# How often GpSimd waits for free slots of the gather ring in the second layer's pass over the edges

## Chip, cores and metric

One NeuronCore of a Trainium2 chip runs the whole program in one launch. The metric is the device time in microseconds. The program is made of Bass instructions: each engine (TensorE or PE, VectorE or DVE, ScalarE or ACT, GpSimd or POOL, SyncE or SP) has its own list, in its own order, and the lists meet only in semaphores.

## What is computed

Two graph-attention layers, each with a residual and a layer norm around it, over 6250 nodes of 128 features and 106250 edges sorted by destination. The change lies in the second layer's pass over the edges, which computes this part of the reference:

```python
x_src = (node_embeddings @ W_src + b_src).reshape(num_nodes, H, D)      # H = 4, D = 32
x_dst = (node_embeddings @ W_dst + b_dst).reshape(num_nodes, H, D)
e = edge_emb[edge_type].reshape(-1, H, D)
combined = jax.nn.leaky_relu(x_src[src] + x_dst[dst] + e, negative_slope=0.2)
logits = jnp.einsum('ehd,hd->eh', combined, att)
mx = jax.ops.segment_max(logits, dst, num_segments=num_nodes)
ex = jnp.exp(logits - mx[dst])
sums = jax.ops.segment_sum(ex, dst, num_segments=num_nodes)
attn = ex / jnp.maximum(sums[dst], 1e-12)
agg = jax.ops.segment_sum(x_src[src] * attn[..., None], dst, num_segments=num_nodes)
```

`x_src[src]` is a gather: for each edge, one row of 132 numbers (528 bytes) is fetched from a table in HBM.

## The kernel before

The program runs in stages: preparing and first tables (`front`), the first layer's pass over the edges (`edges0`), joining and node updates (`join_tiles`, `nodes0`), the second layer's pass (`edges1`), and again joining and node updates (`join_tiles`, `nodes1`).

`edges1` goes over 896 steps of 128 edges. Four steps (QS = 4) make a quad, so there are 224 quads. All five engines run the same loop over quads, each with its own part. Sixteen quads (RQ = 16) are written out in the body of a hardware loop; the first 32 and the last 16 quads stand outside of it. `nth(i, c, per, plus)` turns a quad's number into the count that a semaphore has by then.

The gathered rows live in a ring of 16 quad slots, the tile `rows` (carved from `pair`, the name that the profile shows). A quad passes through it in this way:

- GpSimd, function `gather` (L1803 to L1814): for quad c it waits, at every eighth quad, for the index tile that ScalarE copies (`idx_in`, L1805), then until the slot is free (L1807, `sums`), then adds one to the semaphore `passed` (`apart`, L1808 and L83), for which nobody waits, and issues four indirect DMAs (L1811), one for each step. Each counts up the slot's semaphore `rows_in` by 16 when its rows have landed.
- TensorE, function `edge` (L1976 to L1988): when the slot's rows are in, it adds gathered and destination rows in PSUM (L1985, L1987) and counts `x_summed`.
- VectorE makes logits of them (L1851 to L1870); every eight quads a block of logits is turned, scanned, exponentiated and copied into the last four columns of the rows (L1997, L1891, L1898, L1905, ScalarE L1962, TensorE L2004, ScalarE L1944).
- Ten quads after its logits (LAG = 10), VectorE scales the quad's rows (L1867, semaphore `scaled`) and TensorE sums them into nodes with eight fp32 matmul passes (L2011) in two halves, h = 0 and 1. Each half counts `sums` by one, so quad w is done with its slot when `sums` is 2(w + 1). Each half has one PSUM tile, so TensorE waits before each half of a quad until ScalarE has copied out the same half of the quad before (L2009, semaphore `evicted`).
- ScalarE copies both halves out (L1953); VectorE adds them to the accumulators (L1880).

In iteration c TensorE does `edge(c + 1)` and then the sum of quad w = c - 10. GpSimd's gather of quad g needs the sum of quad g - 16, which TensorE makes in iteration g - 6, and TensorE wants the rows in iteration g - 1, five quads later. The order of the work is written out by hand; there is no planner.

The wait around which the change turns:

```python
if i is not None or c >= RQ:
    pl.wait_ge(sums, nth(i, c - RQ + 1, 2))
apart(pl, k.passed)
```

Of the kernel before, what the change touches and what calls it, by code (L numbers as in the profile page):

```python
# [40 lines left out]
RQ = 16  # L41
# [38 lines left out]
def apart(eng, passed):  # L80


    eng.sem_inc(passed, 1)  # L83
# [1621 lines left out]
def nth(i, c, per=1, plus=0):  # L1705

    v = c * per + plus
    return v if i is None else i * (RQ * per) + v


def edges1(nc, k):
# [8 lines left out]
    with ExitStack() as ctx:  # L1720
# [30 lines left out]
        sums, evicted, added = sem("sums"), sem("evicted"), sem("added")  # L1751
# [4 lines left out]
        def quads(i, c0, emit):  # L1756
            for c in range(c0, c0 + (RQ if c0 else HEAD)):
                emit(i, c)
# [11 lines left out]
        with nc.Block() as block:  # L1770
            @block.sync
            def _(sp):
                sp.dma_start(index1[:, :], k.d_index1).then_inc(index_in, 16)
                sp.dma_start(att[:, :], io["L1_gnn_att"].rearrange("h d -> (h d)").partition_broadcast(P)).then_inc(att_in, 16)

                def group_in(i, c):
                    u = c // LQ % 2
                    g = c // LQ if i is None else i * 2 + c // LQ
                    if i is not None or c >= 2 * LQ:
                        sp.wait_ge(oht_built, nth(i, c - LQ))  # L1780
                    sp.dma_start(node[u][0:BN, :], k.d_node.rearrange("(g s) e -> g (s e)", s=LQ * QS)[bass.ds(g, 1), :]
                                 .broadcast_to([BN, LQ * QS * P])).then_inc(node_in[u], 16)
                    sp.dma_start(node[u][BN:P, :], k.d_type8.rearrange("(g s) e -> g (s e)", s=LQ * QS)[bass.ds(g, 1), :]
                                 .broadcast_to([NT, LQ * QS * P])).then_inc(node_in[u], 16)
                    if i is not None or c >= 2 * LQ:
                        sp.wait_ge(maxed, nth(i, c // LQ - 1) if i is None else i * 2 + (c // LQ - 1))
                    for h in range(H1):
                        sp.dma_start(gate[u][h * LQ * QS:(h + 1) * LQ * QS, :],
                                     k.d_gate[bass.ds(g * (LQ * QS), LQ * QS), :]).then_inc(gate_in[u], 16)

                def emit(i, c):
                    if c % LQ == 0 and live(i, c + LQ):
                        group_in(i, c + LQ)

                group_in(None, 0)
                whole(sp, emit)
                half = S // (4 * QS)
                for u in range(2):
                    sp.wait_ge(bound_out[u], 16 * (half // 2))

            @block.gpsimd
            def _(pl):
                def gather(i, c):  # L1803
                    if c % LQ == 0:
                        pl.wait_ge(idx_in, c // LQ + 1 if i is None else i * 2 + (c // LQ + 1))  # L1805
                    if i is not None or c >= RQ:
                        pl.wait_ge(sums, nth(i, c - RQ + 1, 2))  # L1807
                    apart(pl, k.passed)  # L1808
                    for t in range(QS):
                        r = c % RQ * QS + t  # L1810
                        nc.gpsimd.indirect_dma_start(  # L1811
                            rows[:, r, :], None, k.d_table1,
                            bass.IndirectOffsetOnAxis(ap=idx[c // LQ % 2][:, c % LQ * QS + t:c % LQ * QS + t + 1], axis=0))\
                            .then_inc(rows_in[c % RQ], 16)  # L1814

                quads(None, 0, gather)
                with pl.Fori(0, NITER) as i:
                    quads(i, HEAD, gather)
                quads(None, NQUAD - RQ, gather)
# [632 lines left out]
```

## Time and profile before

| | us |
|---|---|
| median of 3 runs (lowest, highest) | 3859.63 (3853.22, 3862.32) |
| the profiled execution, its own time | 3879.43 |
| its span in the trace | 3877.2 |
| first gather of `edges1` to its last | 2268.6 to 3654.5 |
| gathers of `edges1`: busy us, count, mean ns | 896.3, 896, 1000 |

The page gives busy times for each engine. In the second layer's pass GpSimd does nothing but gathers, and a gather's record covers the work of GpSimd, not the transfer. The tile name `pair` stands for everything carved from that buffer; in a wait the words "DMA pair<-in_xT" mean that the last event which the profile found on a name like this came from a DMA. "issue" is idle time in which the engine waited for nothing that the profile shows.

### The profile page before, as it was taken

The page shows a single profiled execution, that of the slowest core. Times are in us where ns is not written, and L with a number is a line of the kernel's source. Part 1 is how long each engine was busy: PE and PEld are TensorE (multiplying, and loading weights), DVE is VectorE, ACT ScalarE, POOL GpSimd, SP SyncE. Part 2 cuts the span into 40 slices and gives each one's busy share as a digit, 9 for nine tenths or more (in the row PEclk, how much of TensorE's full clock was granted, in tenths as well). Part 3 has the DMA queues.
Part 4 walks back from the last instruction along what each step waited for, and adds up shares of the span by engine and source line. Part 5 has one row for each costly group of instructions (what it writes and reads, how often), then busy time and mean ns, then how long its engine had stood idle before and what let it go on. Part 6 is the DMA issues. An engine that isn't in the chain of part 4 may idle for free. (4 is left out here: it accounts for less than half of the span.)

```text
span 3877.2 us, 61415 instructions
## 1 busy us (share of the span) xinstructions
PE 2638.8 (68%) x13446; PEld 2020.7 (52%) x13447; DVE 2512.7 (65%) x6012; ACT 1132.5 (29%) x3922; POOL 1938.7 (50%) x1981
## 2 busy tenths in 40 slices
PE   6993877776776787777568834566666666656653
PEld 3672655565555565555444424555555555555543
DVE  5443777676776677677755535666666666666768
ACT  2440434343343443344325510111111111111105
POOL 1004455555555555556430045666666666666453
PEclk9896888888888899899789977888778888787865
DMA  5475455555555555555401132333333333333231
GB/s 101 97 209 172 132 146 152 148 150 146 148 145 147 146 153 153 145 149 160 98 3 26 28 73 59 69 67 69 68 68 68 68 68 70 68 68 68 36 51 34
DMA packets 263396, 390.00 MB, mean 101 GB/s; under 512 B 79436, under 2 KB 177895, under 8 KB 259449
## 3 DMA queue, kind: packets, MB, share of 16 engines
q0 software_dynamic: 87584, 242.80, 24.7%
q1 hardware_dynamic: 162789, 138.70, 14.7%
q10 hardware_dynamic: 12788, 6.19, 0.6%
q14 instruction: 187, 1.53, 0.1%
q8 instruction: 48, 0.79, 0.1%
HBM read 346.51 MB, written 40.92 MB: 100 GB/s over the span
## 5 line engine op out<-in xcount | busy, mean ns | idle before, releaser
L1811 POOL DMA_INDIRECT pair<-d_table,e_idx x896 | 896.3, 1000 | 790.7 <-ACT e_idx L1934 300.2
L1095 POOL DMA_INDIRECT pair<-d_table,e_idx x896 | 877.1, 979 | 677.5 <-issue 240.3
L2011 PE MATMUL e_p_r<-pair,e_oh 128*122 128x132 f32 x1792 | 339.0, 342 | 448.1 <-DVE pair L1867 281.5
L1293 PE MATMUL e_p_t<-e_wbd,e_feat 128*128 128x512 f32 x448 | 286.3, 725 | 392.3 <-DVEq L1159 196.2
L2011 PEld LDWEIGHTS e_p_r<-pair,e_oh 128*122 128x122 f32 x1792 | 286.5, 234 | 493.3 <-issue 338.5
L1953 ACT COPY pair<-e_p_r 122x264 f32<-122x264 f32 x448 | 162.8, 379 | 1051.0 <-DMA pair<-in_xT 540.6
L1985 PE MATMUL e_p_x<-pair,iden 128*128 128x264 f32 x896 | 342.7, 471 | 100.0 <-issue 47.4
L1987 PEld LDWEIGHTS e_p_x<-big,e_oht 128*128 128x128 f32 x1792 | 336.2, 232 | 48.6
L1297 PEld LDWEIGHTS e_p_q<-big,e_oht 128*128 128x128 f32 x1792 | 282.4, 225 | 134.1 <-issue 134.1
L1987 PE MATMUL e_p_x<-big,e_oht 128*128 x1792 | 332.2, 317 | 0.0
L1851 DVE SCALAR_TENSOR_TENSOR e_prod<-e_p_x,e_att 128x512 f32<-128x512 f32 x224 | 153.1, 683 | 267.1 <-DMA d_tile_decay<-pair 234.3
L1251 ACT COPY e_bound<-e_p_r 122x272 f32<-122x272 f32 x448 | 158.1, 386 | 560.1 <-remote 357.4
L1305 PEld LDWEIGHTS e_p_m<-big,e_oht 128*128 128x128 f32 x1792 | 243.0, 195 | 137.9 <-issue 137.9
L1880 DVE TENSOR_TENSOR big<-big,pair 120x132 f32 x896 | 219.5, 294 | 122.6 <-ACT pair L1953 75.4
L1293 PEld LDWEIGHTS e_p_t<-e_wbd,e_feat 128*128 128x128 f32 x448 | 76.6, 214 | 416.8 <-issue 237.1
L1150 DVE TENSOR_TENSOR pair<-pair,e_p_t 128x512 f32<-128x512 f32 x224 | 153.9, 687 | 215.5 <-issue 124.8
L1259 ACT ACTIVATE e_p_m<-e_p_m 128x128 f32<-128x128 f32 x896 | 237.4, 265 | 184.3 <-ACT e_bound L1251 83.0
L1139 DVE TENSOR_TENSOR big<-big,e_bound 120x136 f32 x896 | 263.2, 294 | 36.2 <-issue 19.2
L1297 PE MATMUL e_p_q<-big,e_oht 128*128 x1792 | 281.2, 309 | 0.0
L1317 PE MATMUL e_p_r<-pair,e_oh 128*122 128x136 f32 x1792 | 257.2, 287 | 22.6 <-DVE pair L1185 17.2
L1303 PE MATMUL e_p_m<-pair,iden 128*128 128x512 f32 x448 | 257.2, 659 | 0.0
L1155 DVE TENSOR_TENSOR pair<-pair,e_p_q 128x512 f32<-128x512 f32 x224 | 152.6, 681 | 156.6 <-remote 144.2
(365 smaller groups left out, 4605.7 us busy)
## 6 DMA issues: line engine op xcount, KB each, us to landing
pair<-d_table,e_idx POOLq DMA_INDIRECT x1792
e_node<-d_node SPq DMA_DIRECT2D x112, 240.0 KB
e_node<-d_node SPq DMA_DIRECT2D x28, 960.0 KB
d_table<-tab_kmv SPq DMA_DIRECT2D x54, 360.0 KB
e_feat<-in_edge_attr SPq DMA_DIRECT2D x896, 16.0 KB
e_gate<-d_gate SPq DMA_DIRECT2D x448, 8.1 KB
d_decay<-pair SPq DMA_DIRECT2D x7, 512.0 KB
e_decay<-d_decay SPq DMA_DIRECT2D x56, 64.0 KB
```

Source lines behind the costliest of these rows:

```text
L1095: nc.gpsimd.indirect_dma_start(rows[:, c % RQ0 * QS + t, 0:3 * D], None, k.d_table0, bass.IndirectOffsetOnAxis(ap=idx[c // LQ0 % 3][:, c % ...
L1139: last = V.tensor_tensor(to, to, bound[a // BQ % 3][0:BN, a % BQ * QS + t, :].unsqueeze(1), ALU.add)
L1259: last = A.activation(p_m[c % 2][:, t, :], p_m[c % 2][:, t, :], ACT.Square, accum_out=d2[c // LQ0 % 3][:, c % LQ0 * QS + t:c % LQ0 * QS + ...
L1293: M(p_t[:, :, :].rearrange("p t d -> p (t d)"), feat[c % 4][:, :], wbd[:, :, :].rearrange("p t d -> p (t d)"), start=True, stop=True).then ...
L1297: last = M(p_q[:, t, :], oht[c % 3][:, t * P:(t + 1) * P], qm[:, bass.ds(of[t], 1), 0:D], start=True, stop=True)
L1303: M(m[:, :, :], k.iden[:, :], rows[:, r:r + QS, D:2 * D], start=True, stop=False)
L1305: last = M(m[:, t, :], oht[c % 3][:, t * P:(t + 1) * P], qm[:, bass.ds(of[t], 1), D:2 * D], start=False, stop=(t == QS - 1))
L1317: last = M(p_r[h][0:R_LAST + 1, t - 2 * h, 0:W], oh[w % 2][:, t, :], rows[:, w % RQ0 * QS + t, 2 * D:R0], start=True, stop=True)
L1811: nc.gpsimd.indirect_dma_start(rows[:, r, :], None, k.d_table1, bass.IndirectOffsetOnAxis(ap=idx[c // LQ % 2][:, c % LQ * QS + t:c % LQ * ...
L1985: M(x[:, 2 * h:2 * h + 2, 0:W], k.iden[:, :], rows[:, r + 2 * h:r + 2 * h + 2, :], start=True, stop=False)
L1987: last = M(x[:, t, 0:W], oht[c % 4][:, t * P:(t + 1) * P], xd[:, bass.ds(held["blocks"][(c - 1) % 4 * QS + t if c else t], 1), :], start=F ...
L2011: last = M(p_r[h][0:R_LAST + 1, t - 2 * h, 0:W], oh[w % 2][:, t, :], rows[:, w % RQ * QS + t, :], start=True, stop=True)
```

## The change

GpSimd waits for the ring and counts `passed` at even quads only. At an even quad c it waits until `sums` says that quad c - 15 (and so quad c - 16 too) is done, and then issues the eight gathers of quads c and c + 1 one after the other. For the first 16 quads there is still no wait for the ring. The wait for the index tile, at every eighth quad, stays. No other engine's list is touched.

```diff
                 def gather(i, c):
                     if c % LQ == 0:
                         pl.wait_ge(idx_in, c // LQ + 1 if i is None else i * 2 + (c // LQ + 1))
-                    if i is not None or c >= RQ:
-                        pl.wait_ge(sums, nth(i, c - RQ + 1, 2))
-                    apart(pl, k.passed)
+                    if c % 2 == 0 and (i is not None or c >= RQ):
+                        pl.wait_ge(sums, nth(i, c - RQ + 2, 2))
+                    if c % 2 == 0:
+                        apart(pl, k.passed)
                     for t in range(QS):
                         r = c % RQ * QS + t
                         nc.gpsimd.indirect_dma_start(
```

## Rows read from the trace of the kernel before

**Rows 1.** The page: the span.
```profile
span 3877.2 us, 61415 instructions
```

**Rows 2.** Busy time by stretch: us, engines' busy us (count), PEclk, DMA share, GB/s.
```profile
2413.00:3640.00 1227.00, 764.24 (x4053) 672.17 (x4053) 809.53 (x2076) 165.92 (x500) 797.30 (x800) 0.81 0.31 67
...
3660.00:3705.00 45.00, 36.26 (x158) 31.14 (x158) 38.24 (x106) 11.91 (x33) 0.00 (x0) 0.61 0.01 2
```

**Rows 3.** Waits in 2413 to 3640 us: engine, line, releaser: total us, times, longest.
```profile
ACT pair L1953 <- DMA pair<-in_xT: 510.1, 92, 11.9
...
POOL pair L1811 <- issue: 220.1, 693, 2.9
...
POOL pair L1811 <- DMA pair<-in_xT: 148.9, 59, 3.2
...
POOL pair L1811 <- PE e_p_r L2011: 61.2, 48, 2.5
```

**Rows 4.** Groups by line, 2413 to 3640 us: busy us, mean ns, idle before.
```profile
L1811 POOL DMA_INDIRECT pair<-d_table,e_idx x800 | 797.4, 997 | 430.1 <-issue 220.1 <-DMA pair<-in_xT 148.9 <-PE e_p_r L2011 61.2
L1985 PE MATMUL e_p_x<-pair,iden 128*128 128x264 f32 x800 | 304.9, 469 | 13.2 <-issue 9.8 <-DVE e_oht L1838 3.1
```

**Rows 5.** GpSimd in order of time: start us, duration us, [idle before, releaser].
```profile
2839.88 1.28 POOL L1811 DMA_INDIRECT pair<-d_table,e_idx  x1 [0.30 <-issue]
2843.19 0.94 POOL L1811 DMA_INDIRECT pair<-d_table,e_idx  x1 [2.03 <-DMA pair<-in_xT]
...
2855.44 0.94 POOL L1811 DMA_INDIRECT pair<-d_table,e_idx  x1 [2.05 <-DMA pair<-in_xT]
```

**Rows 6.** TensorE in order of time, the same stretch.
```profile
2837.51 1.16 PE L2011 MATMUL e_p_r<-pair,e_oh 128*122 128x132 f32 x8 [0.34 <-DVE pair L1867]
...
2842.77 1.39 PE L2011 MATMUL e_p_r<-pair,e_oh 128*122 128x132 f32 x8 [2.31 <-ACT pair L1953]
...
2847.39 1.16 PE L2011 MATMUL e_p_r<-pair,e_oh 128*122 128x132 f32 x8
...
2855.12 1.24 PE L2011 MATMUL e_p_r<-pair,e_oh 128*122 128x132 f32 x4 [2.15 <-ACT pair L1953]
...
2867.36 2.05 PE L2011 MATMUL e_p_r<-pair,e_oh 128*122 128x132 f32 x8 [3.89 <-ACT pair L1953]
```

**Rows 7.** ScalarE in order of time, the same stretch.
```profile
2842.34 0.66 ACT L1953 COPY pair<-e_p_r 122x264 f32<-122x264 f32 x2 [7.98 <-DMA pair<-in_xT]
...
2851.83 0.38 ACT L1953 COPY pair<-e_p_r 122x264 f32<-122x264 f32 x1 [7.25 <-DMA pair<-in_xT]
2854.69 0.66 ACT L1953 COPY pair<-e_p_r 122x264 f32<-122x264 f32 x2 [2.48 <-DMA pair<-in_xT]
2856.39 0.38 ACT L1953 COPY pair<-e_p_r 122x264 f32<-122x264 f32 x1 [1.05 <-PE e_p_r L2011]
...
2866.93 0.66 ACT L1953 COPY pair<-e_p_r 122x264 f32<-122x264 f32 x2 [6.20 <-DMA pair<-in_xT]
```

**Rows 8.** TensorE and ScalarE after the last gather, in order of time.
```profile
3672.30 1.16 PE L2011 MATMUL e_p_r<-pair,e_oh 128*122 128x132 f32 x8 [0.61 <-DVE pair L1867]
3673.05 0.83 ACT L1953 COPY pair<-e_p_r 122x264 f32<-122x264 f32 x2 [2.74 <-PE e_p_r L2011]
```

**Rows 9.** GpSimd in order of time: twelve gathers in one burst, and the break behind.
```profile
2978.79 0.94 POOL L1811 DMA_INDIRECT pair<-d_table,e_idx  x1 [2.15 <-DMA pair<-in_xT]
...
2992.96 0.94 POOL L1811 DMA_INDIRECT pair<-d_table,e_idx  x1 [0.30 <-issue]
2996.92 1.21 POOL L1811 DMA_INDIRECT pair<-d_table,e_idx  x1 [3.02 <-DMA pair<-in_xT]
```

**Rows 10.** GpSimd in order of time: the ring's first wait, first and last counted gather.
```profile
2382.55 0.94 POOL L1811 DMA_INDIRECT pair<-d_table,e_idx  x1 [27.12 <-PE e_p_r L2011]
...
2412.89 0.94 POOL L1811 DMA_INDIRECT pair<-d_table,e_idx  x1 [2.83 <-DMA pair<-in_xT]
...
3654.46 0.94 POOL L1811 DMA_INDIRECT pair<-d_table,e_idx  x1 [0.30 <-issue]
```

## The prediction

> **What bounds the kernel now.** I read the stretches first. From 2413 to 3640 us all five engines loop over the quads of the second layer, and none is full: TensorE works 764, VectorE 810, GpSimd 797 of 1227 us [rows 2]. That is a loop held by waits. The 812 gathers that start from 2412.89 to 3654.46 us [rows 10] are 203 quads in 1242.5 us, so 6.12 us a quad. The table of groups says that TensorE does not wait for gathered rows: 13.2 us idle ahead of 800 instructions of L1985 [rows 4]. GpSimd does wait for slots: 430 us idle ahead of 800 gathers [rows 4], of which 210 us in 107 pauses are not plain issue time [rows 3]. So the ring is full, and what frees the slots, the chain of TensorE's sums and ScalarE's copies, sets the pace.
>
> The list of waits then has an odd entry: ScalarE's copy L1953 waits 510 us, 92 times, "for a DMA" [rows 3], though it mostly waits for `sums`, which TensorE counts. In order of time: TensorE's sum of one quad is recorded from 2837.51 to 2838.67 [rows 6], ScalarE copies it at 2842.34 [rows 7], 3.7 us late, and GpSimd, which needs the same count, goes on at 2843.19, 0.85 us after ScalarE [rows 5]. GpSimd's last gather had ended at 2841.16. The next sum but one ends at 2848.55 [rows 6]; its halves are copied at 2851.83 and 2854.69 [rows 7], and GpSimd goes on at 2855.44, 2.05 us after it had fallen silent [rows 5]. After the last gather this never happens: sum at 3672.30, copy at 3673.05, during the sum's last matmuls [rows 8]. I read it so: while GpSimd issues gathers in a long burst, TensorE's counts reach the others late, mostly only when GpSimd has paused for 1 to 2 us. The label "DMA" is what stands at the time of release, not what is waited for.
>
> Burst by burst, for the 32 sums from 2800 to 3000 us (four of them in [rows 6]): where the first half ended less than 4.8 us into a burst, 11 of 12 were on time; later than that, 19 of 20 were late. Cut at breaks over 1 us, the 812 gathers are 86 bursts: 51 of eight (10.21 us, then a break of 2.15 us on average), 31 of twelve (15.32 and 2.86), three of four gathers and one of twenty (break 3.07); one of eight stands between 2843.19 and 2855.44 [rows 5], one of twelve in [rows 9]. Eight cost 12.36 us for two quads, 6.18 each; twelve cost 18.18 us, 6.06 each.
>
> **The change part by part.**
>
> *Taken away:* 104 waits and 112 counts of `passed` on GpSimd. The gap between two gathers is 0.30 us with or without them between (693 gaps, 220.1 us [rows 3]). Nobody waits for `passed`. Worth nothing: at most 104 x 0.02 us = 2 us if the wait itself shows.
>
> *Added:* at an even quad GpSimd waits for quad c - 15 instead of c - 16. Behind this wait stand the eight gathers, and behind them TensorE's wait for rows. These rows have cover: TensorE wants them five quads (5 x 6.12 = 30.6 us) after the slot is free, with the change four (24.5 us) for an even quad, and a burst of eight with its break takes 12.36 us. Cost of a late landing: nothing. Without that cover, up to one quad a pair, 104 x 6.12 = 636 us. The first such wait moves from the first sum, which started GpSimd at 2382.55 [rows 10], to the second: some 3 us, once, and covered in the same way.
>
> *The burst's start.* The two sums of a pair come together or apart. If the late one is the odd quad's, the even one's has long arrived, and the change alters nothing: GpSimd starts 0.85 us after the release. If the late one is the even quad's, the odd quad's sum can only begin after the release, since its PSUM tile is still to be copied: release 2842.34, sum 2842.77 to 2844.16; release 2854.69, second halves until 2856.36; release 2866.93, sum 2867.36 to 2869.41 at the lower clock [rows 6, 7]. That is 1.8, 1.7 and 2.5 us, mean 2.0 us, by which GpSimd starts later than now.
>
> *How often.* After a burst whose late sum was odd, the next even sum is made at once. The next odd one ends some 6 us after the release, 4.9 us into the new burst as in [rows 5, 6], just at the limit, where it is now late in 51 and on time in 31 of 82 bursts. If late, the cycle repeats as now (12.36 us). If on time, both sums are there when GpSimd asks, and the burst goes on to sixteen; the next even sum falls 9 us into it and is late. Sixteen gathers take 15.32 x 16 / 12 = 20.4 us, the break I put at 3.1 us (between 2.86 after twelve and 3.07 after twenty), and here the 2.0 us are paid: 25.5 us for four quads. The next burst then starts so late that the following even sum ends 3 us into it (on time), the odd one 7 us into it (late): 12.36 us, and the kernel is back at the start. On average 51/31 = 1.65 plain cycles, one of sixteen and one more of eight: 20.4 + 25.5 + 12.4 = 58.3 us for 3.3 + 4 + 2 = 9.3 quads, 6.26 us each, against 6.12 now. Over the 208 quads that wait for the ring: 0.14 x 208 = 29 us.
>
> On the break after a burst, the Trainium skill ("DMA: Bandwidth & Descriptors", section "Queues, rings and completion order") says that a DMA's semaphore increment is an ordered write, landing only after all earlier writes of that DMA engine. That fits breaks which grow from 2.15 to 3.07 us with the burst. By its fixed 2.0 us per DMA (section on the anatomy of one DMA), plus the 0.85 us, every break would be 2.85 us by estimate, and the sum 5 us less through the break after sixteen; the measured breaks decide.
>
> *Bounds.* If no even sum is ever the late one: 0. If it always is, every pair pays: 104 x 2.0 = 208 us. Below nothing: if bursts of sixteen come without that price, (20.4 + 3.1) / 4 = 5.88 us a quad, 50 us less over all 208. I take 29, near the side of nothing, because the late sum shifts to the odd quad by itself after one burst.
>
> Sum: 3879.4 (the profiled execution; its span is 3877.2 [rows 1]) + 29 = 3908. The timed runs have their median at 3859.6, 20 us below the profiled execution, so 3859.6 + 29 = 3889.
>
> **The rivals.**
>
> *No change (3860).* The chain of sums and copies may have its own pace. Then the burst's start does not matter, or the lateness settles on the odd quads and never pays. For it: TensorE hardly waits for rows [rows 4], so a gather 2 us later harms nobody by itself. Against it: releases follow GpSimd's pauses, and a later burst ends later. The Trainium skill ("Perfetto Trace Analysis", summary of the profiler window per engine type) says that a matmul's end in the profile is an estimate and the semaphore's way is hidden; by that, the sums could simply end later than recorded, whatever GpSimd does, and the time stay at 3860.
>
> *Faster (3835).* Long bursts are the cheaper ones, 6.06 against 6.18 us a quad. If the pair's wait makes sixteens common and the late sum is odd, half of the quads at 5.88 save 0.24 x 104 = 25 us. It decides from the point where the second odd sum ends under 4.8 us into its burst.
>
> *Slower by far (3960 to 4068).* The even sum stays late in half or all of the pairs: 52 to 104 x 2.0 = 104 to 208 us. It needs even sums more than 4.8 us into the burst, where after a delayed start they should be at 3. One variant: TensorE starts to wait for rows.
>
> *The change doesn't bite:* where GpSimd now finds both sums there, as in each burst of twelve for one pair or so, nothing is different. That is in the sum already.
>
> **How the numbers follow.** Forecast 0.50, no change 0.24, faster 0.17, far slower 0.09. Differences of 0.2% (8 us) are about what this kernel's timing can tell from none. The forecast's own range is 3867 to 3930 (nothing paid in most sixteens, or the 2.0 us paid in every third pair, 70 us); a tenth of it falls within 0.2%, and so does part of the other two: faster 0.17, same 0.25, slower 0.58. For 8 in 10 the range goes from 3840 to 3945.
>
> **What would show it.** In the changed kernel's trace GpSimd's breaks stand only before even quads, so bursts are of eight and sixteen; twelves are gone. Some breaks are near 4 us, where TensorE's L2011 ended 0.8 us before the gather; the others stay at 2 to 3 us. L1811's idle in the pass grows by some 30 us, L1985 still waits for almost nothing, and everything before 2382 us and after the pass is as before. The forecast is wrong if breaks over 3.5 us are missing, if L1985 begins to wait for rows, or if TensorE's counts are as late with GpSimd silent as with it busy.

## Result, and the profile after

The changed kernel takes 3917.40 us (median of four runs, 3893.27 to 3922.31), the kernel before 3856.43 us in four runs (3836.09 to 3862.32): ratio 1.0171, 95% interval 1.0136 to 1.0206, so 61 us slower. The forecast was 29 us slower. The direction was right; the size was too small by half. TensorE's granted clock was 0.836 in both profiled executions, and 0.81 and 0.80 in the stretch below, so the clock is not what changed. In two of the five sets of runs below the kernel before itself took 3355 to 3359 us; why is open, and every run is given against the kernel before of its own set.

The page's span, and its group of GpSimd's gathers in the second pass:

```profile
span 3920.1 us, 61215 instructions
...
L1812 POOL DMA_INDIRECT pair<-d_table,e_idx x896 | 892.5, 996 | 863.5 <-ACT e_idx L1935 301.1
```

The span grew by 42.9 us [rows 1]; the profiled run of before lay 20 us over its median. The pass itself, from first gather to last, took 1454.0 us (the times stand in the head of the view of L1812) against 1385.9, which is 68.1 more. It began 15.7 us earlier in this execution, and what follows it was 9.5 us shorter.

```profile
L1812 POOL DMA_INDIRECT pair<-d_table,e_idx x896: 938/944/7786, 2252.9 to 3706.9; - x180
```

The stretch 2413 to 3640 us again, busy times first (columns as in [rows 2]), then the waits, then the groups:

```profile
2413.00:3640.00 1227.00, 717.60 (x3847) 626.83 (x3847) 768.33 (x1972) 156.37 (x474) 750.51 (x757) 0.80 0.31 65
```

```profile
ACT pair L1954 <- DMA pair<-in_xT: 547.3, 77, 17.4
...
POOL pair L1812 <- issue: 225.3, 684, 7.8
DVE e_prod L1852 <- DMA d_tile_decay<-pair: 201.0, 36, 13.1
POOL pair L1812 <- PE e_p_r L2012: 190.6, 46, 11.0
...
POOL pair L1812 <- DMA pair<-in_xT: 60.6, 27, 3.2
```

```profile
L1812 POOL DMA_INDIRECT pair<-d_table,e_idx x757 | 750.5, 991 | 476.4 <-issue 225.3 <-PE e_p_r L2012 190.6 <-DMA pair<-in_xT 60.6
L1986 PE MATMUL e_p_x<-pair,iden 128*128 128x264 f32 x760 | 287.7, 467 | 25.7 <-issue 15.8 <-DVE e_oht L1839 6.5 <-DMA pair<-d_table,e_idx 2.8
```

In the same 1227 us GpSimd issued 757 gathers where it had issued 800 [rows 2]. A gather costs what it cost (991 ns against 997 [rows 4]) and the idle time between neighbours is the same (225.3 us against 220.1 [rows 3]). What grew is the idle time until a sum arrives: 190.6 + 60.6 = 251 us in 73 pauses, where it had been 210 us in 107 [rows 3], and for fewer gathers. TensorE still does not wait for rows (25.7 us before L1986, of which 2.8 for the gathers).

Cut into bursts at breaks over 1 us, the gathers of the changed kernel are these (the last burst has no break behind it; lengths and breaks are means):

| kernel | four | eight (length + break) | twelve | sixteen | per quad |
|---|---|---|---|---|---|
| before | 3 | 51 (10.21 + 2.15) | 31 (15.32 + 2.86) | none (one of twenty, 3.07) | 6.12 us |
| after | none | 47 (10.15 + 2.25) | none | 27 (20.52 + 6.19) | 6.45 us |

The twelves are gone and only eights and sixteens are left, as forecast. An eight costs 12.40 us for two quads (12.36 before). A sixteen costs 26.7 us for four quads, 6.68 each, and there the time is. This is one of them, GpSimd in order of time:

```profile
2725.03 0.94 POOL L1812 DMA_INDIRECT pair<-d_table,e_idx  x1 [1.81 <-PE e_p_r L2012]
...
2744.14 0.94 POOL L1812 DMA_INDIRECT pair<-d_table,e_idx  x1 [0.30 <-issue]
2753.18 0.94 POOL L1812 DMA_INDIRECT pair<-d_table,e_idx  x1 [8.10 <-PE e_p_r L2012]
```

and the other engines inside it (start, duration, engine, line):

```profile
2733.11 1.16 PE L2012 MATMUL e_p_r<-pair,e_oh 128*122 128x132 f32 x8 [1.21 <-issue]
...
2737.98 1.09 PE L1988 MATMUL e_p_x<-big,e_oht 128*128 x4
...
2747.69 0.69 DVE L1852 SCALAR_TENSOR_TENSOR e_prod<-e_p_x,e_att 128x512 f32<-128x512 f32 x1 [13.08 <-DMA d_tile_decay<-pair]
2747.88 0.66 ACT L1954 COPY pair<-e_p_r 122x264 f32<-122x264 f32 x2 [17.35 <-DMA pair<-in_xT]
...
2749.47 0.68 DVE L1868 TENSOR_TENSOR pair<-pair 128x512 f32<-128x512 f32 x1
...
2750.28 2.11 PE L2012 MATMUL e_p_r<-pair,e_oh 128*122 128x132 f32 x8 [11.21 <-DVE pair L1868]
...
2752.43 0.38 ACT L1954 COPY pair<-e_p_r 122x264 f32<-122x264 f32 x1 [0.50 <-PE e_p_r L2012]
```

TensorE finishes the even quad's sum at 2734.27, 9.2 us into the burst, and goes silent at 2739.07. Neither count is acted upon: ScalarE (L1954, which needs `sums`) copies the sum 13.6 us after it ended, VectorE (L1852, which needs TensorE's `x_summed`) goes on 8.6 us after TensorE fell silent. (Their idle times, 17.35 and 13.08 us, also hold time before the work they wait for was done.) GpSimd falls silent at 2745.08; 2.6 and 2.8 us later VectorE and ScalarE go on, almost together. Only then can VectorE scale the odd quad (L1868, 2749.47), TensorE sum it (2750.28 to 2752.39), and GpSimd start at 2753.18, 5.3 us after the release and 8.10 after it fell silent. Before the change a release let GpSimd go within 0.85 us [rows 5, 7].

### The profile page after: what moved, and what is told of

The parts are those of the page before. It is cut to its first block and busy times, and to the rows that moved or that the text cites. A ratio compares the mean times of both kernels' runs of the same rounds, so it can differ in the third digit from the quotient of the medians.

```text
span 3920.1 us, 61215 instructions
## 1 busy us (share of the span) xinstructions
PE 2633.9 (67%) x13446; PEld 2009.9 (51%) x13447; DVE 2512.7 (64%) x6012; ACT 1130.7 (29%) x3922; POOL 1944.8 (50%) x1981
## 3 DMA queue, kind: packets, MB, share of 16 engines
q10 hardware_dynamic: 12788, 6.19, 0.6%
## 5 line engine op out<-in xcount | busy, mean ns | idle before, releaser
L1812 POOL DMA_INDIRECT pair<-d_table,e_idx x896 | 892.5, 996 | 863.5 <-ACT e_idx L1935 301.1
L1095 POOL DMA_INDIRECT pair<-d_table,e_idx x896 | 886.7, 990 | 641.0 <-issue 245.8
L2012 PE MATMUL e_p_r<-pair,e_oh 128*122 128x132 f32 x1792 | 325.1, 333 | 445.8 <-DVE pair L1868 268.4
L2012 PEld LDWEIGHTS e_p_r<-pair,e_oh 128*122 128x122 f32 x1792 | 273.8, 225 | 489.9 <-issue 305.7
L1954 ACT COPY pair<-e_p_r 122x264 f32<-122x264 f32 x448 | 162.1, 380 | 1089.2 <-DMA pair<-in_xT 590.0
L1986 PE MATMUL e_p_x<-pair,iden 128*128 128x264 f32 x896 | 340.5, 468 | 113.7 <-issue 53.4
L1852 DVE SCALAR_TENSOR_TENSOR e_prod<-e_p_x,e_att 128x512 f32<-128x512 f32 x224 | 153.4, 685 | 313.0 <-DMA d_tile_decay<-pair 274.2
```

Of the source, the lines that this page charges most:

```text
L1095: nc.gpsimd.indirect_dma_start(rows[:, c % RQ0 * QS + t, 0:3 * D], None, k.d_table0, bass.IndirectOffsetOnAxis(ap=idx[c // LQ0 % 3][:, c % ...
L1812: nc.gpsimd.indirect_dma_start(rows[:, r, :], None, k.d_table1, bass.IndirectOffsetOnAxis(ap=idx[c // LQ % 2][:, c % LQ * QS + t:c % LQ * ...
L1986: M(x[:, 2 * h:2 * h + 2, 0:W], k.iden[:, :], rows[:, r + 2 * h:r + 2 * h + 2, :], start=True, stop=False)
L2012: last = M(p_r[h][0:R_LAST + 1, t - 2 * h, 0:W], oh[w % 2][:, t, :], rows[:, w % RQ * QS + t, :], start=True, stop=True)
```

## The experiments

All are timed against the kernel before on the same chip. A quad is called late where ScalarE begins to copy its first half over 0.5 us after the recorded end of TensorE's sum of that half. Of quads 20 to 199 that is 89 of 180 before and 80 after. Where many are late, I say that counts are held; this is a name for what the records show, since the recorded end of a matmul is modelled and a sum that was really finished late would look the same.

### More of the same: one wait per four quads

```diff
-                    if c % 2 == 0 and (i is not None or c >= RQ):
-                        pl.wait_ge(sums, nth(i, c - RQ + 2, 2))
-                    if c % 2 == 0:
+                    if c % 4 == 0 and (i is not None or c >= RQ):
+                        pl.wait_ge(sums, nth(i, c - RQ + 4, 2))
+                    if c % 4 == 0:
```

> Theory L (TensorE's counts reach the other engines late once GpSimd has issued gathers for about 5 us in a row, and come through only some 2 to 3 us after it stops): all bursts are now of sixteen gathers (20.5 us). The first sum falls early into the burst and is on time, the second is held until 2.6 us after its end, and the third and fourth then follow at about 4 us each, so a burst and its break take some 32 us for four quads, 8.0 us a quad against 6.12: about 390 us more than the kernel before (some 4250 us), and breaks of 9 to 13 us. Rival T (the sums and copies have their own pace of 6.1 us a quad, whatever GpSimd does): four quads still take 24.5 us, and the time stays within 30 us of the changed kernel's 3917.

Measured 4131.58 against 3837.84 us, ratio 1.0767 (1.0723 to 1.081). GpSimd's waits from 2400 to 3900 us:

```profile
POOL pair L1812 <- PE e_p_r L2012: 456.0, 47, 11.3
```

Every burst is a sixteen (50, the last aside), 20.25 us long, and every break is long: 9.61 us on average, 7.47 us a quad. Of the four sums that GpSimd then needs, two (31 times) or three (19 times) are copied in full only after it has fallen silent. In the changed kernel it needs two, so there it is at most two. Sign and mechanism hold; the size was 294 us where 390 had been expected.

### Half the gathers in each quad

Both kernels gather only steps 0 and 2 of each quad (the other two keep old rows), and the waits of ScalarE and TensorE for a quad's rows count two landings instead of four; everything else runs as it was.

```diff
-                    for t in range(QS):
+                    for t in range(0, QS, 2):
```

> The kernel before, but steps 1 and 3 of each quad of the second layer are not gathered (two gathers a quad, the rest of the work as it was on whatever lies in the slots). Theory L: GpSimd is busy 2.5 us a quad, bursts stay under 5 us, counts arrive on time, and the loop runs at VectorE's some 4.0 to 4.3 us a quad: 370 to 440 us less than before, 3420 to 3490 us. Rival T: the pace stays near 6.1 us and the time near 3856.

> The changed kernel (one wait for two quads), with steps 1 and 3 of each quad not gathered, so a pair is four gathers, 5 us. Theory L: the lateness needs longer bursts than this, so the pair's wait costs little: within 30 us of the kernel with half of the gathers and a wait for each quad. If it were instead the later start of the pairs that costs by itself (rival S), the same 61 us would show here as well.

3485.34 us (ratio 0.9084, 0.9045 to 0.9123) and 3498.62 (0.9118, 0.908 to 0.9156), both against 3837.84. One count late of 180, and 3 of 180. ScalarE's copies of the first of the two, 2350 to 3250 us:

```profile
L1953 ACT COPY pair<-e_p_r 122x264 f32<-122x264 f32 x391 | 145.9, 379 | 668.3 <-PE e_p_r L2011 618.1 <-issue 34.9 <-DVEq L1908 6.5
```

The releaser "DMA" has vanished from this row (510 us before [rows 3]); what is left are waits that end with TensorE's L2011, the line it had been waiting for all along. Nothing is held where bursts are of two gathers (mostly) or of four. The second pass takes 1021.0 and 1022.8 us, so there the pair's wait costs nothing that can be seen; the 13 us between the two medians are hardly clear of the spread of four runs. The pace, 4.58 us a quad, is above the 4.0 to 4.3 that had been expected of VectorE.

### Landing ahead of the next burst

The changed kernel, with a wait of GpSimd for the rows of quad c - 1 before an even quad's eight gathers. This forces a break after each eight.

```diff
+                    if c % 2 == 0 and (i is not None or c >= RQ):
+                        b = c - 1
+                        pl.wait_ge(rows_in[b % RQ], 16 * QS * (b // RQ + 1) ...)
                     if c % 2 == 0 and (i is not None or c >= RQ):
```

> The changed kernel, with one more wait at each even quad: GpSimd waits until the rows of the quad it has just issued have landed, so a break of about 2 us stands after every eight gathers and no burst of sixteen is possible. Theory L, with the loss in the bursts of sixteen (6.66 us a quad against 6.20 for the eights): most of the 61 us come back, 3860 to 3885 us. Rival S (each pair's later start costs by itself, or any wait added to GpSimd costs): it stays at 3917 or goes above it.

A miss: 3930.21 against 3837.84, ratio 1.0228 (1.0185 to 1.0271). The sixteens are gone (101 bursts of eight), but each break is 2.83 us, so a pair takes 10.21 + 2.83 = 13.04 us, 6.52 a quad, and now TensorE starves, which neither theory had:

```profile
L1989 PE MATMUL e_p_x<-pair,iden 128*128 128x264 f32 x752 | 318.2, 514 | 369.8 <-issue 307.4 <-DVE e_oht L1842 35.7 <-DMA pair<-d_table,e_idx 26.2
```

369.8 us idle before L1989 (13.2 [rows 4] before). The profile puts 307.4 of them down to nothing it shows; they are waits for rows that came too late. In 79 of quads 20 to 199 TensorE starts on a quad's rows within 1.75 us of the end of the quad's last gather, never sooner than 1.56 us; in the kernel before the shortest such lead is 10.9 us. The wait for the ring no longer holds GpSimd either: it starts each pair at least 8.2 us after the sum that it needs. So GpSimd with its own waits for landings sets the pace here, at 13.04 us a pair, and only 41 of 180 sums being late did not help. The run says nothing of a sixteen's price; it shows that a certain break of 2.83 us after each eight costs as much as what the change brought.

### Is it the bytes, or GpSimd being busy?

Three kernels on one chip, before at 3896.55 us. First, rows of 132 bytes in place of 528 (the table is addressed as rows of 33 numbers, so the same row numbers fetch a quarter of the bytes, from the table's first quarter):

```diff
-                            rows[:, r, :], None, k.d_table1,
+                            rows[:, r, 0:33], None, k.d_table1.rearrange("n (a b) -> (n a) b", b=33),
```

> The kernel before, but each gather of the second layer fetches rows of 33 numbers (132 bytes) instead of 132 numbers; as many gathers and as many rows in each. Theory I (the counts are held by the issuing of many gathers in a row, so by their number): bursts, breaks and the time stay as before, within 25 us. Rival D (held by the bytes that are moved): the counts are on time, and the pass is held by GpSimd's four gathers alone, 5.1 to 5.4 us a quad against 6.12, 150 to 210 us less than before.

3886.45 us, ratio 0.998 (0.9952 to 1.0008): nothing. 96 of 180 late, and the bursts as before (6, 47 and 33 of four, eight and twelve, with breaks of 2.07, 2.07 and 2.97 us).

```profile
L1953 ACT COPY pair<-e_p_r 122x264 f32<-122x264 f32 x398 | 144.6, 382 | 946.9 <-DMA pair<-in_xT 433.0 <-PE e_p_r L2011 381.4 <-issue 129.2
```

Second, `half_before` with GpSimd kept busy in place of each gather left out, by a memset that nobody reads (1280 columns, 1.18 us):

```diff
+                    if i is not None or c >= 1:
+                        pl.wait_ge(paused, nth(i, c, 2))
+                    for t in range(0, QS, 2):
...
+                        nc.gpsimd.memset(idle[:, t // 2, :], 0.0).then_inc(paused, 1)
```

> The kernel before with two gathers a quad (steps 1 and 3 not gathered, as in half_before), and behind each of them a write of 1280 columns by GpSimd that nobody reads, some 1.3 us, so that GpSimd is as busy as with four gathers. Theory I: the counts stay on time (at most a tenth of the quads late), and a quad takes what GpSimd takes, about 5.1 us: 80 to 180 us above half_before's 3485. Rival B (the counts are held by GpSimd being busy, whatever with): late counts in about half of the quads and the pace of before, 6.1 us a quad, 3820 to 3860 us.

3721.12 us (0.9545, 0.9503 to 0.9587), and none of 180 late. The groups of GpSimd and ScalarE, 2413 to 3500 us:

```profile
L1818 POOL MEMSET pair<- 128x1280 f32 x398 | 469.8, 1180 | 0.3
L1814 POOL DMA_INDIRECT pair<-d_table,e_idx x398 | 413.2, 1038 | 205.4 <-POOL pair L1818 163.9 <-issue 38.0 <-PE e_p_r L2015 3.5
...
L1957 ACT COPY pair<-e_p_r 122x264 f32<-122x264 f32 x394 | 147.6, 380 | 850.1 <-PE e_p_r L2015 630.3 <-issue 204.0 <-DVEq L1912 8.4
```

GpSimd works 883 of 1087 us here, 81%, against 65% before [rows 2], and no count is held: ScalarE's waits for a sum end with the sum (L2015). So it is neither the bytes nor a busy GpSimd; what remains is gathers issued back to back, or many of them in a stretch of time. (This kernel has half the gathers in all, so the runs don't tell the one from the other.) A quad takes 5.45 us, not the 5.1 that had been expected.

Third, a memset of 512 columns (0.53 us) ahead of each quad's four gathers:

```diff
+                    if i is not None or c >= 1:
+                        pl.wait_ge(paused, nth(i, c))
...
+                    nc.gpsimd.memset(idle[:, :], 0.0).then_inc(paused, 1)
                     for t in range(QS):
```

> The kernel before, but GpSimd writes 512 columns that nobody reads ahead of each quad's four gathers: a pause in the gathers of some 0.8 us for each quad. If a pause this short lets the held counts through, bursts of gathers end after 5 us, nothing is late, and a quad takes 5.1 + 0.8 = 5.9 us: some 45 us less than before. If it doesn't (theory I with a release that needs 1 to 2 us of silence), the breaks stay and the pauses come on top: 6.7 to 6.9 us a quad, 120 to 160 us more.

3876.84 us, 0.9942 (0.9916 to 0.9967): 20 us faster, neither of the two sizes that had been expected. 86 of 180 stayed late, and bursts grew up to 24 gathers long. Half a microsecond between quads does not let the counts through, yet it takes nothing from the pace.

### VectorE's work, and a condition in which no count is held

In `light_*` VectorE's one-hot (L1856) is made for two quads only and the add into the accumulators (L1880) left out, which takes 317 us of work from VectorE (2491.1 busy in `after_3`, 2173.7 in `light_after`); in `pause_after` and `pause_short` the memset stands in the changed kernel (512 columns; `passed` is counted at every quad again there) and in the one before (256).

```diff
-                        V.tensor_tensor(oh[w % 2][:, :, :], ..., ALU.is_equal)
+                        if i is None and w < 2:
+                            V.tensor_tensor(oh[w % 2][:, :, :], ..., ALU.is_equal)
...
-                        v.did(V.tensor_tensor(to, to, bound[a // 4 % 2][0:BN, a % 4 * QS + t, :].unsqueeze(1), ALU.add))
```

> The kernel before with 1.6 us less for VectorE in each quad of the second layer: the one-hot tiles (L1856) are built for the first two quads only, and the additions into the accumulators (L1880) are left out. Theory I (GpSimd's bursts hold TensorE's counts): VectorE's work is not what sets the pace, bursts and late counts stay, and a quad takes 5.9 to 6.1 us, 0 to 40 us less than before. If VectorE's 4 us a quad were the real bound, 200 us or more would go.

> The changed kernel with the same VectorE work left out. Theory V (in the bursts of sixteen whose break is 7.8 us, VectorE too had been held, and had to go through a quad after the release before TensorE could make the odd quad's sum): these long breaks go, the mean break after sixteen falls from 6.2 to about 5.2 us, and the difference to light_before is 20 to 45 us. Rival (the long breaks come from TensorE or ScalarE alone): the mean break stays at 6 us or more and the difference at 60 us.

> The changed kernel with GpSimd's write of 512 columns ahead of each quad, which for the kernel before took 0.6% off. Theory I: the pause lets a part of the held counts through, so the pair's wait costs no more than without it: 20 to 60 us above pause_before. If the pair's wait cost only through bursts without any pause, it would be within 10 us of pause_before.

> The kernel before with 256 columns, half of pause_before's, written ahead of each quad. Theory I: a shorter pause lets less through but also takes 0.25 us less from GpSimd a quad: between before and pause_before, 5 to 25 us less than before. If any gap of a different kind is enough, it is better than pause_before, 40 us or more less than before.

Here the kernel before itself took 3358.54 us, 479 to 538 less than in the sets above, on the very chip that had given 3896.55. In the traces of these four no sum was late (0 of 180), GpSimd never paused over 0.31 us in the pass, and the pass of `light_before` took 1156 us, where that of before takes 1386. Against 3358.54: `light_before` 3342.57 (0.9949, 0.9925 to 0.9973), `light_after` 3336.59 (0.9934, 0.9909 to 0.996), `pause_after` 3454.05 (1.0286, 1.0245 to 1.0327), `pause_short` 3395.21 (1.0111, 1.0069 to 1.0152). Nothing of what was expected can be read from them, since each expectation rested on held counts. They do show GpSimd as the bound when nothing is held: VectorE's relief brings half a percent, and a memset costs about what it takes. Before a quad's first gather stand 0.54 + 0.17 us where 0.30 had stood, so 0.41 x 224 = 92 us, measured 96 (from `pause_after`):

```profile
2500.52 0.54 POOL L1812 MEMSET pair<- 128x512 f32 x1
2501.23 1.00 POOL L1815 DMA_INDIRECT pair<-d_table,e_idx  x1 [0.17 <-POOL pair L1812]
2502.53 0.94 POOL L1815 DMA_INDIRECT pair<-d_table,e_idx  x1 [0.30 <-issue]
```


The light pair was run again on another chip, with the changed kernel beside it, and the counts were held there (before at 3846.64):

> The changed kernel once more. In the last four runs no count was late and GpSimd never paused, and the kernel before took 3358 us in place of 3840 to 3900. If the counts are held here (kernel before near 3850): 45 to 75 us more than before, as first measured. If they aren't (kernel before near 3360): GpSimd's gathers follow each other without a break in both kernels, a slot is always free when it is asked for, and the pair's wait costs nothing: within 8 us of the kernel before.

> As light_before (VectorE's one-hot tiles and additions left out), again since no count was held there. Where counts are held, theory I: late counts in about half of the quads, 0 to 40 us less than the kernel before. Where they aren't: 16 us less, as measured.

> As light_after, again. Where counts are held, theory V: the mean break after sixteen gathers falls from 6.2 to about 5.2 us, and the difference to light_before_2 is 20 to 45 us; the rival: break 6 us or more and 60 us. Where they aren't: within 8 us of light_before_2.

| kernel | us | ratio (95%) | eights | twelves | sixteens | late |
|---|---|---|---|---|---|---|
| `after_2` | 3918.58 | 1.0176 (1.0148 to 1.0203) | 38 (2.14) | none | 31 (5.76) | 69 |
| `light_before_2` | 3805.36 | 0.9872 (0.9845 to 0.9899) | 20 (2.15) | 48 (2.80) | 5 (3.04) | 87 |
| `light_after_2` | 3867.22 | 1.0049 (1.0023 to 1.0074) | 14 (2.21) | none | 43 (4.98) | 92 |

(Counts of bursts, with the mean break behind them in us.) The changed kernel repeats its 1.7%. The breaks after a sixteen come in three kinds, told apart by what was still to do at the release:

| at the release | after | `after_2` | `light_after_2` |
|---|---|---|---|
| the odd quad still to be scaled by VectorE | 12, 7.80 us | 10, 8.17 | 4, 7.77 |
| it was scaled, its sum still to be made | 11, 5.53 | 13, 5.64 | 28, 5.27 |
| the odd quad was the late one | 4, 3.18 | 8, 2.93 | 11, 3.20 |

With less to do, VectorE is less often caught with the scaling undone (4 of 43, not 12 of 27 or 10 of 31), and the mean break falls from 5.76 to 4.98 us, close to the 5.2 that had been expected of it. The three prices hardly move; their shares do. `light_before_2` is 41 us faster than the kernel before, at the edge of the 0 to 40 expected. But the pair's wait costs 62 us between the two light kernels, where the theory of VectorE's share gave 20 to 45, so its size is a miss. The sixteens became frequent (43 of 57); I take it that the shorter break was spent on more of them, which no run shows by itself. The row of its waits, GpSimd from 2413 to 3640 us in `light_after_2`, still has 249 us of waits:

```profile
L1812 POOL DMA_INDIRECT pair<-d_table,e_idx x776 | 756.5, 975 | 470.9 <-issue 221.5 <-PE e_p_r L2011 199.0 <-DMA pair<-in_xT 50.5
```

Last, the changed kernel where nothing is held. On one more chip before took 3355.38 us:

> The changed kernel a third time. Where the kernel before takes some 3360 us (no count held): within 8 us of it, and no pause of GpSimd over 1 us in the pass. Where it takes 3840 to 3900 us: 45 to 75 us more than it.

> GpSimd's write of 512 columns ahead of each quad, again. Where the counts are held: 10 to 30 us less than the kernel before, as measured. Where they aren't, GpSimd's own work sets the pace and the write comes on top: 224 quads x 0.45 us, some 80 to 110 us more (pause_short with half the columns had 37 us more there).

The changed kernel took 3357.42: ratio 1.0005 (0.9984 to 1.0026). The memset kernel took 3449.15, 1.0269 (1.0235 to 1.0303), where it had been 0.6% faster with held counts. GpSimd's waits (2120 to 3100 us) and the page's groups of the changed kernel there:

```profile
POOL pair L1812 <- issue: 222.8, 731, 0.3
POOL pair L1812 <- PE e_p_r L2012: 7.3, 24, 0.3
```

```profile
L1812 POOL DMA_INDIRECT pair<-d_table,e_idx x896 | 896.5, 1001 | 576.9 <-ACT e_idx L1935 304.1
...
L1954 ACT COPY pair<-e_p_r 122x264 f32<-122x264 f32 x448 | 167.5, 378 | 869.4 <-PE e_p_r L2012 856.5
```

In 980 us GpSimd never idles longer than the 0.3 us between two gathers; the pass takes 1168.4 us, and 896 x (1.001 + 0.30) is 1166. GpSimd is the bound, at 5.2 us a quad, and ScalarE's waits end with TensorE's L2012. So the change costs nothing by itself, wait, burst and late landing together: -5 to +9 us. What it cost elsewhere it cost only where counts were held. This also limits the mechanism: long bursts are not enough for it. The first layer's pass, which gathers in the same way (L1095), is shorter in this condition as well: 1249 us from first gather to last, not the 1546 of the kernel before. This is also why `half_before`, whose first pass was as long as ever (1516 us), is slower in all than the whole kernel is here.

## Why the prediction was half right

*What bounds the kernel:* right as far as the runs go. The chain of sums and copies, held by GpSimd's bursts, set the pace; with short bursts the lateness went away (1 of 180) and with it 9.2% of the time, with bytes cut to a quarter it stayed. That counts come through only after GpSimd pauses is true of most, not of all: 61 of the 89 late ones before were copied in a break, 28 during a burst.

*Removed wait, landing cover:* right. L1986 lost 2.8 us to gathered rows in the stretch, and `after_3` puts all of the change at 2 us, from -5 to +9. The cover did get thin: the shortest time from a quad's last gather to TensorE's use of it fell from 10.9 to 3.7 us.

*How often:* nearly right. Forecast 2.65 eights for a sixteen, measured 47 to 27, 1.74. At the forecast's durations this mix gives (47 x 12.36 + 27 x 25.5) / 202 quads = 6.28 us a quad, not 6.26: some 5 us of the pass. The limit of 4.8 us from which it was reasoned came from 32 sums and is less sharp over the whole pass: judged by the first half, 60 of 63 sums that ended sooner in a burst were on time, but so were 31 of 117 that ended later or in the break. And the even sum did not fall 9 us into each sixteen but 9.1 to 14.1.

*The price of a sixteen:* the step that failed, in the term called the burst's start. The break was put at 3.1 us plus 2.0 us for an odd sum that can begin at the release. Measured: 6.19 us over 27 sixteens, so 27 x (6.19 - 5.1) = 29 us, and 27 x 0.12 = 3 us for a burst of 20.52 us where 20.4 stood. The 2.0 us were read from sums for which VectorE had already scaled the quad [rows 6]. In a sixteen VectorE is held too, by TensorE's other count (`x_summed`), so in 12 of 27 cases the odd quad is still to be scaled at the release: 4.25 us from ScalarE's copy of the even quad's second half to the end of the odd sum, and 7.80 us of break. In 11 cases with the quad scaled it is 2.33 and 5.53 us, 0.4 above the 5.1. Four sixteens had a late odd quad and paid no second sum (3.18, the forecast's 3.1). Against 5.1 us the three kinds make +32, +5 and -8 us: the quad left unscaled accounts for all of the 29. The row for this stood in the same table of waits of the kernel before as [rows 3], and I passed it by, with an odd releaser of the same kind for a wait on TensorE:

```profile
DVE e_prod L1851 <- DMA d_tile_decay<-pair: 166.7, 33, 7.9
```


The sum: 29 (forecast) + 32 (price of a sixteen) + 5 (mix) + 47 x 0.04 = 2 (eights) = 68 us, and the pass grew by 68.1. So close a match is in part luck of rounding, and it holds for one execution only; the medians give 61.

*The rivals:* "no change" fell where counts are held and is what `after_3` shows where they are not; its stated reason (the chain has a pace of its own) is not the one at work there, since GpSimd is then the bound. "Faster" fell: sixteens did become common, but an even sum was the late one in 23 of 27. "Slower by far" did not come either; `four`, where held sums follow one another in each break, shows what it would have looked like.

*By the Trainium skill:* the estimate of 2.85 us for every break, from the fixed 2.0 us of "DMA: Bandwidth & Descriptors" (section on the anatomy of one DMA), does not agree with the breaks of 2.15 us after eight. The page speaks of a DMA's own completion, and these breaks are no waits for one; where GpSimd does wait for a landing (`land_after`), the median break is 2.4 us. The Trainium skill ("Perfetto Trace Analysis", summary of the profiler window per engine type) has the end of a matmul as an estimate; by that the lateness could be a fault of the record. `half_before` and `half_busy` speak against a mere fault of the record: there the same records of the same matmuls show 1 and 0 late, and the time fell. They do not tell counts that travel late from sums that TensorE really finished late while gathers were issued.

## What stays open

What holds the counts. The runs narrow it to gathers issued back to back, whatever their bytes, and to a condition that was absent in two sets of runs, one of them on a chip that had shown it in the set before. No run here varies that condition. Whether TensorE's counts travel late or its sums are finished late is open too. Only what TensorE tells the others was seen to be late, not what they tell it: where TensorE waited for a scaling by VectorE that ended over 5 us into a burst, it began the sum within 0.14 us, 49 of 49 times before and 57 of 57 after.

## To carry to other kernels

The wait moved to a coarser grain cost nothing here where its engine was the bound and the counts came at once (`after_3`); it cost where work could only follow the release, one link after the other. So ask for each grouped wait how many links of the chain can only run after the engine has fallen silent. Price such a break with every engine that was held, not the one in whose row it was first seen. When a releaser's name makes no sense, compare the wait with what the program waits for.

## What the hardware did unexpectedly

While GpSimd issued gathers for over some 5 us without a break, counts of TensorE mostly reached ScalarE, VectorE and GpSimd late: ScalarE copied a half sum up to 8.8 us after its recorded end before the change and up to 14.1 us after it. Two thirds of the late ones (61 of 89 before, 56 of 80 after) came through in a break. Over eight kernels the first late copy of such a break began 1.0 to 1.3 us after GpSimd stopped on average where the burst had been of eight gathers, 1.9 to 2.2 after twelve, and 2.1 to 2.3 after sixteen, the single ones at up to 3.0 us. VectorE's counts reached TensorE within 0.14 us in the same bursts, and so did ScalarE's in the seven cases of the two kernels that show it. In the condition without lateness the same program takes 3355 to 3359 us in place of 3838 to 3897. With single gathers and memsets in turn nothing was held (0 of 180); a memset of 0.53 us at every fourth gather was not break enough (86 of 180).
